# Edge attention of layer 1: probabilities with sources on partitions, for three destination tiles at a time

## What is computed

```python
def _gat_conv(x, W, a_src, a_dst, b, src, dst, n):
    xw = x @ W
    e = jax.nn.leaky_relu((xw @ a_src)[src] + (xw @ a_dst)[dst], 0.2)
    m = jax.ops.segment_max(e, dst, num_segments=n)
    ex = jnp.exp(e - m[dst])
    s = jax.ops.segment_sum(ex, dst, num_segments=n)
    alpha = ex / (s[dst] + 1e-16)
    agg = jax.ops.segment_sum(alpha[:, None] * xw[src], dst, num_segments=n)
    return agg + b

x = jax.nn.relu(_gcn_conv(event_emb, W1, b1, src, dst, n))
x = jax.nn.relu(_gat_conv(x, W2, att_src, att_dst, b2, src, dst, n))
```

## Time and profile before

| | us |
|---|---|
| median of three runs | 2361.07 (2360.67 to 2363.16) |
| the profiled execution, its time | 2366.88 |
| its span in the trace | 2365.1 |
| PE busy in the span | 1997.1 (84%) |
| DVE busy | 1474.2 (62%) |
| ACT busy | 1036.3 (44%) |
| POOL busy | 551.5 (23%) |
| `gat_ps_o` matmuls (L2851), 1250 passes | 273.9 |
| `gat_ps_t` transposes (L2844), 625 | 74.6 |

### The profile page before, as it was taken

The page is one execution under the profiler, slowest core; times in us unless marked ns, Lnnn a source line. Parts: engine busy times, 40 slices in busy tenths (PEclk is TensorE's granted clock), DMA queues, the critical chain, the costliest instruction groups (busy, mean ns, idle before and its releaser), DMA issues. The chain is left out here.

```text
span 2365.1 us, 41463 instructions
## 1 busy us (share of the span) xinstructions
PE 1997.1 (84%) x12047; PEld 1624.9 (69%) x12047; DVE 1474.2 (62%) x3791; ACT 1036.3 (44%) x1835; POOL 551.5 (23%) x612
## 2 busy tenths in 40 slices
PE   6938888878877758998697898769999965999998
PEld 3526666656633447998365776569888854999997
DVE  3479999978832655554565322399999656444443
ACT  3525555545511524665351343166666430333332
POOL 1000000047611734554310000000000001454443
PEclk9979999977898559999798999989999956999999
DMA  2014334330077301221502342212121081633332
GB/s 69 0 46 133 117 121 129 109 93 1 1 168 211 103 25 54 71 71 54 127 0 54 95 136 63 56 42 65 53 66 53 0 291 54 195 79 75 49 47 33
DMA packets 90653, 189.74 MB, mean 80 GB/s; under 512 B 14121, under 2 KB 58432, under 8 KB 90570
## 3 DMA queue, kind: packets, MB, share of 16 engines
q1 hardware_dynamic: 72906, 157.31, 23.0%
q0 software_dynamic: 17664, 31.47, 6.4%
HBM read 124.22 MB, written 64.52 MB: 80 GB/s over the span
## 5 line engine op out<-in xcount | busy, mean ns | idle before, releaser
L2224 PEld LDWEIGHTS experts_ps_h<-experts_xt,experts_up 128*128 128x128 f32 x2944 | 351.8, 194 | 10.3 <-issue 3.3
L2224 PE MATMUL experts_ps_h<-experts_xt,experts_up 128*128 128x128 f32 x2944 | 353.0, 277 | 3.0 <-DVE experts_xt L2346 1.8
L2851 PE MATMUL gat_ps_o<-Y,gat_prob_t 125*125 125x256 f32 x1250 | 273.9, 379 | 0.0
L2851 PEld LDWEIGHTS gat_ps_o<-Y,gat_prob_t 125*125 125x125 f32 x1250 | 232.7, 188 | 33.7
L1233 PE MATMUL adj_ps_w<-adj_one_k,adj_one_s 128*125 128x500 bf16 x1000 | 178.8, 305 | 78.6 <-DVE adj_one_k L1164 56.0
L2236 PE MATMUL experts_ps_o<-experts_down,experts_hid 128*128 128x256 f32 x960 | 226.7, 379 | 0.0
L2284 ACT ACTIVATE experts_down<-down 128x1024 f32 (+1 forms) x120 | 138.8, 1157 | 175.7 <-DVE experts_out L2334 77.1
L2316 DVE COPY experts_up<-up 128x1024 f32 (+1 forms) x184 | 123.1, 698 | 112.8 <-issue 68.8
L1233 PEld LDWEIGHTS adj_ps_w<-adj_one_k,adj_one_s 128*125 128x125 bf16 x1000 | 98.3, 138 | 128.6 <-DVE adj_one_k L1164 60.2
L2236 PEld LDWEIGHTS experts_ps_o<-experts_down,experts_hid 128*128 128x128 f32 x960 | 173.2, 190 | 18.7
L1177 ACT ACTIVATE adj_tile<-adj_ps_w 125x500 bf16<-125x500 f32 x250 | 95.8, 438 | 150.1 <-PE adj_ps_w L1233 150.1
(11 more groups left out here) (436 smaller groups left out, 3783.9 us busy)
## 6 DMA issues: line engine op xcount, KB each, us to landing
adjacency<-adj_tile SPq DMA_DIRECT2D x25, 683.6 KB
adjacency_t<-adj_tile_t SPq DMA_DIRECT2D x25, 683.6 KB
adj_in<-adjacency_t SPq DMA_DIRECT2D x25, 683.6 KB
QT<-adjacency SPq DMA_DIRECT2D x25, 683.6 KB
cnt<-adjacency_t SPq DMA_DIRECT2D x25, 683.6 KB
up<-in_L_ffn_w SPq DMA_DIRECT2D x32, 512.0 KB, 6.3
down<-in_L_ffn_w SPq DMA_DIRECT2D x16, 512.0 KB, 7.1
up<-in_L_ffn_W SPq DMA_DIRECT2D x8, 512.0 KB, 6.2
```

Source lines behind the costliest of these rows:

```text
L2224: last = nc.tensor.matmul(ps[:, h * 128:(h + 1) * 128], w[:, k * H + h * 128:k * H + (h + 1) * 128], xt[b][:, k, :], start=(k == 0), stop= ...
L2851: last = nc.tensor.matmul(ps_o[b][0:ROWS, 0:C], prob_t[:, s * ROWS:(s + 1) * ROWS], K.Y[:, s, :], start=(s == 0), stop=(s == TILES - 1))
```

## The change

In the projection, DVE makes a second dot product per tile, with `att_src`, so that the sources' terms also stand one per partition (`K.AT_SRC`). `K.Y` becomes `K.Y_one`, 257 columns wide, the last of ones, so that the weighted matmul gives the sum of the weights in its last column.

In `gat`, the score pass stays for each tile, but only its two shifts are kept. Tiles are taken in nine groups, the first of one tile and eight of three. POOL sets the shifts on a diagonal, PE multiplies a matrix of ones with it, so that every partition holds the shifts of all destinations as a row (`rows`), and DVE copies these out of PSUM (`copy_rows`, `ab`). The work then goes in units of five source tiles by the group's destinations (125x1875, or 125x625 in the first group), five units a group, 45 in all: ACT makes both exponentials, source tile by source tile, with the source's term as the bias per partition, into `once` (three buffers) and `fifth` (two); DVE takes the minimum with 1 and the greater of both (`greater`); POOL multiplies by the counts, now from `adjacency`, which SP loads as well, three tiles a group into two buffers (`weigh`); PE uses the result as weights as it stands, 15 matmuls a unit (`unit`). A table of three small dictionaries says after which unit DVE makes the next score passes, PE the next rows and DVE the copies. ACT refills a `once` buffer when PE has finished the unit three back (`unit_done`) and DVE the maximum two back (`maxed`). The core of the diff:

```diff
             for u in range(GROUP):
...
+                    nc.vector.tensor_tensor_reduce(out=src_prod[:, u, :], in0=bank, in1=at_src[0:ROWS, :], scale=1.0, scalar=0.0,
+                                                   op0=ALU.mult, op1=ALU.add,
+                                                   accum_out=src_dots[:, u:u + 1]).then_inc(y_used, 1)
...
+    groups = [(0, 1)] + [(a, a + 3) for a in range(1, TILES, 3)]
+    NG, UNITS, SPAN = len(groups), 5, TILES // 5
...
+        for u, t in ((0, 1), (1, 2), (2, 3)):
+            scores_after[0, u] = t
+        rows_after[0, 4] = copies_after[0, 4] = 1
+        for u in range(UNITS):
+            scores_after[1, u] = 4 + u
...
+            def greater(g, u):
+                k, wide = UNITS * g + u, SPAN * size(g) * ROWS
+                dve.wait_ge(exped, k + 1 + START)
+                v.tensor_scalar(fifth[k % 2][:, 0:wide], fifth[k % 2][:, 0:wide], 1.0, None, ALU.min)
+                dve.drain()
+                v.scalar_tensor_tensor(once[k % 3][:, 0:wide], once[k % 3][:, 0:wide], 1.0, fifth[k % 2][:, 0:wide],
+                                       ALU.min, ALU.max).then_inc(maxed, 1)
...
+            def weigh(g, u):
+                n, k = size(g), UNITS * g + u
+                pool.wait_ge(maxed, k + 1 + START)
...
+                for i in range(n):
+                    last = p.tensor_tensor(e[:, :, i, :], e[:, :, i, :], adj[g % 2][:, i, u * SPAN:(u + 1) * SPAN, :],
+                                           ALU.mult)
+                last.then_inc(weighed, 1)
...
+                    if k >= 3:
+                        act.wait_ge(unit_done, k - 2 + START)
+                    if k >= 2:
+                        act.wait_ge(maxed, k - 1 + START)
+                    for s in range(SPAN):
...
+                        nc.scalar.activation(once[k % 3][:, part], ab[g % 2][:, 0, 0:wide], ACT.Exp,
+                                             bias=K.AT_SRC[:, at:at + 1])
+                        last = nc.scalar.activation(fifth[k % 2][:, part], ab[g % 2][:, 1, 0:wide], ACT.Exp,
+                                                    bias=fifth_src[:, at:at + 1])
...
+            def unit(g, u):
+                n, k = size(g), UNITS * g + u
+                pe.wait_ge(weighed, k + 1 + START)
```

More of the change, by code:

```diff
@@ L2667, in gat @@
         cnt = K.cnt
+        spare = K.XN[:].rearrange("p t c -> p (t c)")
+        score = spare[:, 0:NODES]
+        full = SPAN * 3 * ROWS
+        once = [m.sb(f"once{i}", (ROWS, full)) for i in range(3)]
+        fifth = [spare[:, NODES:NODES + full], m.sb("fifth", (ROWS, full))[:]]
+        adj = [m.sb(f"adj{i}", (ROWS, 3, TILES, ROWS), BF16) for i in range(2)]
+        ab = [m.sb(f"ab{i}", (ROWS, 2, 3 * ROWS)) for i in range(2)]
+        diag = [m.sb(f"diag{i}", (ROWS, 2, ROWS)) for i in range(3)]
@@ L2681, in gat @@
-        block = m.block()
[L2683 to L2689, removed]
+        adj_in = [m.sem(f"adj_in{i}") for i in range(2)]
+        b_in, fifth_ready, masked, shifted, diag_done, rows_done, copied, own_added = (
+            m.sem(n) for n in ("b_in", "fifth_ready", "masked", "shifted", "diag_done", "rows_done", "copied",
+                               "own_added"))
@@ L2691, in _, with size, landed @@
+        def size(g):
+            return groups[g][1] - groups[g][0]
+        def landed(g):
+            return START + 32 * sum(size(h) for h in range(g % 2, g + 1, 2))
         @block.sync
@@ L2854, in _, with rows @@
-            two_by_two(pe, TILES, tile)
+            def rows(g):
+                if g:
+                    pe.wait_ge(copied, g + START)
+                for i, t in enumerate(range(*groups[g])):
+                    pe.wait_ge(diag_done, t + 1 + START)
+                    for n in range(2):
+                        last = nc.tensor.matmul(ps_r[n][0:ROWS, i * ROWS:(i + 1) * ROWS], K.ones[0:ROWS, 0:ROWS],
+                                                diag[t % 3][:, n, :], start=True, stop=True)
+                last.then_inc(rows_done, 1)
@@ new lines, in unit @@
+            def unit(g, u):
+                n, k = size(g), UNITS * g + u
+                pe.wait_ge(weighed, k + 1 + START)
+                if u == 0 and g >= 2:
+                    pe.wait_ge(evicted, g - 1 + START)
+                for s in range(SPAN):
+                    at = u * SPAN + s
+                    for i in range(n):
+                        last = nc.tensor.matmul(ps_o[g % 2][0:ROWS, i * 512:i * 512 + C + 1],
+                                                once[k % 3][:, (s * n + i) * ROWS:(s * n + i + 1) * ROWS],
+                                                K.Y_one[:, at, :], start=(at == 0), stop=(at == TILES - 1))
+                last.then_inc(unit_done, 1)
@@ L2857 @@
+            rows(0)
+            for g in range(NG):
+                for u in range(UNITS):
+                    unit(g, u)
+                    if (g, u) in rows_after:
+                        rows(rows_after[g, u])
 class Kept:
```

266 lines of the change are left out of this document (128 added, 138 removed).

## The result

The changed kernel takes 2486.4 us (median of four runs, 2484.2 to 2491.9) where the kernel before takes 2361.2 in the same comparison: 1.053 times as long, with an interval of 1.051 to 1.055, or +125 us. The forecast was 2525 us, +164, in a range of 2445 to 2590. The direction and the mechanism hold; the size is 39 us too large. Medians in this document leave out executions in the chip's slower state, of which there was one, of the last kernel (3435 us).

The account below looks back on a forecast made before the run. PE was taken to bound layer 1's edge attention before; after, DVE 277 + POOL 217 in turns, +13 ends, -29 start-ups, +40 ring, +5 clock make 523 us against 364; with +4 projection, 2525 us, range 2445 to 2590.

Parts of the forecast that it names:

- The bound before, and POOL as the cost: Layer 1 edge attention: PE bounds at 13.6 us a tile, DVE close behind; POOL's new work adds to DVE's.
- DVE, 277 us and 25 to 40 out of PSUM: Edge attention: DVE's score passes, minimum, maximum and residual add take 277 us; evictions, PSUM row copies and gaps 25 to 40.
- POOL, 217 us: Edge attention: POOL's 125 count multiplications at 1.50 us, plus own-loop adds and diagonals, take 217 us.
- Turns for the whole instruction, the reduction among them: Edge attention: DVE and POOL share a port and alternate whole instructions, long reduction included, so 277 + 217 = 494 us.
- Rival (b): Edge attention: only DVE's long reduction escapes the port shared with POOL; about 2487 us in total, chance 0.10.
- Rivals (a) and (c): Edge attention: first, DVE and POOL overlap freely, 2390 us, chance 0.10; second, free port, DVE alone bounds, 2331, 0.04.
- Hidden start-ups, -29: Edge attention: blocked DVE or POOL instructions spend 0.13 us of start-up while waiting, on half of some 450: -29 us.
- The ring, +40: Edge attention: three `once` buffers, refilled only after PE finishes the unit three back, starve DVE and POOL: 5 us a group, +40.
- Ends: Edge attention: start (first rows, copies, exponentials, about 5 us) and end (last PE unit 6.6, eviction 2) outside the shared path: +13.
- PE's clock, +5: Edge attention: after idling, PE begins some units at the low clock level, 0.50; +5 us, from 0 to 20.
- Rival (d): Edge attention: PE stays at the low clock, 13.2 us a unit; 2596 us in total, chance 0.06.
- The projection, +4: Projection: a second DVE dot product of 0.42 us a tile adds 4 us, between 0 and 10.

Follow-up runs that it names:

- the last kernel: Changed kernel with multiplication, folded clamps on DVE; mask, eviction, row copies on ScalarE; bias in projection, rows earlier: 2347.4 us, 0.9943 of the kernel before.
- the experiment: Kernel before plus five POOL multiplications a tile that nobody waits for: 2470.1 us with a bf16 factor, 2487.0 with fp32, against 2358.2.
- The bf16 runs: The changed kernel, 2486.4 us, and the kernel before with 125 added POOL multiplications by a bf16 factor, 2470.1 us.
- the fp32 run: Kernel before plus 125 POOL multiplications by an fp32 factor that nobody waits for: 2487.0 us against 2358.2.
- the bf16 variant: Kernel before plus 125 POOL multiplications by a bf16 factor that nobody waits for: 2470.1 us against 2358.2.

## Why the prediction was right, and where its size came from

- **The bound before, and POOL as the cost.** Right. DVE's work was under a microsecond a tile shorter than PE's, and DVE and POOL together passed PE at once: 125 multiplications beside the old kernel cost 112 us.
- **DVE, 277 us and 25 to 40 out of PSUM.** Right as work: the shortest durations add to 300.5, of which 22.6 read PSUM. The sum left these out, as work that can run beside POOL, but only 2.5 us of it did: without it the union would be 16.4 us shorter. The minimum takes 1.12, the maximum 2.11 (1.15 and 2.11 forecast).
- **POOL, 217 us.** This term was mis-sized: 187.8. The step was "take 1.50, since fp32 two-input rows are the nearest". A bf16 factor takes 1.31 in the changed kernel, beside 1.50 for fp32 in the experiment. That is 24 us of the error, and own loops and diagonals at 0.38 and 0.59, for 0.46 and 0.72, another 5. The Trainium skill (GPSIMD Engine Reference, 3.1 Elementwise — side-by-side cycle accounting) has about 2.6 cycles an element for two inputs, by an estimate 1.35 us for 625 at its 1.2 GHz, and gives no price by type. The bf16 runs agree (1.29 to 1.36), the fp32 run does not (1.50).
- **Turns for the whole instruction, the reduction among them.** Right, and with no exception in the rows: 16 of the 25 reductions take some 4.3 us in place of 3.42, and all 18 in the stretch of the experiment. Rival (b) gives the right time for the wrong reason; that the forecast's own errors bring the result to its number is chance. Rivals (a) and (c), which need the two side by side, fall with it.
- **Hidden start-ups, -29.** Right: 195 lengthened instructions by the 0.14 between 1.32 alone and 1.18 behind DVE's end are 27 us by estimate. The records give about as much, 2.5 of their 27 from instructions that read PSUM beside POOL.
- **The ring, +40.** Wrong, the second mis-sized term. The step was "least where no score pass lies between; I take 5 us a group". A unit's trip is covered by the turns themselves, as a slower shared path gives the ring more time (with less on that path it costs some 2 us a unit in the last group, above). A fourth buffer gives 2.8 us, and not by shorter gaps. What idles is 19.4 us in two hand-overs of the rows, for the most part a wait on PE's order that the prediction did not look for (10.5 came back with the rows earlier). Ends: 13 forecast, and the rows give about 4 at the start, 7.40 and 3.1 at the end.
- **PE's clock, +5.** About right by an estimate, but inside the hand-overs. The granted clock is 0.57, 0.76 and 0.86 in the first three stretches; PE holds DVE up for more than 2 us in the two hand-overs and at the end alone. From 1573.2 to 1580.4 and from 1636.4 to 1644.6 us, ahead of the row matmuls, it is 0.61 and 0.79. Passes start 0.43 us apart at the low level there and 0.22 at the full one, so some 2.7 and 1.8 of the 5.25 and 8.98 us are the clock's. No run changed the clock, so this is not shown by itself. At the end the clock is 1.00: the 7.40 us are 0.7 in which PE finishes the unit before and 6.7 for the last one, which I put at 6.6. Rival (d) falls: PE is idle for a quarter of the middle.
- **The projection, +4.** 2.7.

The sum, redone with what was measured: the 488 us of shortest durations, less 17 by which successive records of one engine overlap and 27 of hidden start-ups, make the 444 that the union shows. With 19.4 in the two hand-overs, 14.6 in other long gaps, half of it at the end, and 7.6 in short gaps, most of them of a tenth or less, that is 486. The forecast of 523 was too high by 29 for POOL, by 26 for the ring and the clock, and by the 17 of overlapping records; against that stand 24 for the work out of PSUM that the sum left out, 2 of start-ups, and 9 of ends and short gaps that it had too low. So 72 us too high and 35 too low partly cancel, and the forecast missed by less than its two mis-sized terms make together. A group of three in the middle takes 53.5 to 54 us in the mean of five; 58 was the forecast.

## What to carry to other kernels

An idle GpSimd is not a free engine beside a busy VectorE: where VectorE's instructions read two SBUF tensors, work that reads SBUF there is to be counted into VectorE's own sum, at GpSimd's price. What to move off VectorE in such a stage goes to ScalarE, or into another instruction's second operation. And a number that agrees is no proof of its cause: the rival that gave the right microsecond here was refuted by one line's minimum and median.

## What the runs showed of the hardware

- The shared path is held against the shortest instruction as well: a sum of two [125, 1] columns, 0.16 us alone, takes 1.11 behind a POOL multiplication, and 0.71 in the mean in the kernel before with POOL work added.
- Memsets on POOL, 0.62 us for 125x625, run beside DVE's two-input passes at no cost to either. It was otherwise beside a mask pass, which has one input in bf16: the pass waited for two memsets (1.87 us in place of 0.98), and the next memset waited for the pass (1.44).
- The type of the second operand changes POOL's price, not its use of the path: 1.36 us for 625 elements with a bf16 factor, 1.50 with fp32.
- Where both always have work queued, DVE and POOL alternate instruction by instruction: no instruction of the changed kernel's stage is held for more than one turn. So a long DVE pass makes every POOL instruction behind it as long: the median multiplication of the bf16 variant took 4.40 us.
